# Expert tiles of a vision tower: first product and row turning as pairs over 64 rows, second product over 128

## What is computed

```python
D = 192; M = 768; G = 4; E = 8                       # 32 experts
h = gelu(einsum('nd,edm->enm', xf, W1[g]) + b1[g])   # first product, 192 -> 768
o = einsum('enm,emd->end', h, W2[g]) + b2[g]         # second product, 768 -> 192
y = y + einsum('end,ne->nd', o, combine[:, g, :])    # weighted sum into the token's row
```

## Time and profile before

| | |
|---|---|
| median of 3 runs | 782.18 us |
| span of the profiled execution | 782.1 us (the profile gives no time around it) |
| expert loop, first product of the first tile to that of the last | 399.7 to 768.0 us |
| PE busy in that stretch | 363.5 of 368.3 us |
| typical time from one tile's first product to the next one's | 4.53 us |

### The profile page before, as it was taken

How to read it: one execution, slowest core, us unless ns; L and a number is a source line. 1 busy time by engine, 2 the same in 40 slices (tenths; PEclk the granted TensorE clock), 3 DMA queues, 4 the chain that set the end, 5 groups by cost and what they waited for, 6 DMA issues and landing times.

```text
span 782.1 us, 19902 instructions
## 1 busy us (share of the span) xinstructions
PE 672.5 (86%) x6348; PEld 571.2 (73%) x6348; DVE 426.2 (55%) x1247; ACT 236.5 (30%) x673; POOL 323.5 (41%) x265
## 2 busy tenths in 40 slices
PE   5957858898989996863379899999999999999995
PEld 5724646656745885753269789999999999999994
DVE  7574583745479559977934344444444434434342
ACT  3112312123247211111433333333343333333331
POOL 4730730011023322520334456555564655655554
PEclk9976968577999998975579999999999999999998
DMA  9900000000000030013116765464545665565432
GB/s 349 255 2 3 3 3 2 3 1 3 1 1 1 1 122 1 1 68 132 30 31 164 217 170 116 119 182 81 164 113 161 172 169 161 115 163 114 103 50 38
DMA packets 34982, 70.05 MB, mean 90 GB/s; under 512 B 6353, under 2 KB 21234, under 8 KB 34930
## 3 DMA queue, kind: packets, MB, share of 16 engines
q0 software_dynamic: 15840, 17.71, 13.5%
q10 hardware_dynamic: 8064, 33.12, 12.6%
q1 hardware_dynamic: 11026, 18.48, 7.3%
HBM read 59.31 MB, written 9.98 MB: 89 GB/s over the span
## 4 chain that ended last, share of the span: by engine, by line
PE 62%; DVE 17%; DMA 6%; issue 4%; POOL 1%; ACTq 1%; ACT 1%; DVEq 0%; POOLq 0%
PE bank L1492 17%; PE bank L1484 12%; PE bank L1487 7%; PE bank L1340 4%; PE bank L1469 3%; PE bank L1272 3%; PE bank L1292 3%; DMA arena<-normed_rows,fetch_u 3%; PE bank L1356 2%; DMA out_dram<-arena,number_u 2%; PE bank L1310 1%; PE bank L1283 1%; DVE zx L894 1%; DVE arena L1097 1%; DVE arena L1094 1%
## 5 line engine op out<-in xcount | busy, mean ns | idle before, releaser
L631 POOL DMA_INDIRECT out_dram<-arena,number_u x80 | 127.0, 1587 | 51.6 <-DMA out_dram<-arena,number_u 26.3
L625 POOL DMA_INDIRECT arena<-normed_rows,fetch_u x80 | 78.3, 979 | 114.9 <-DMA out_dram<-arena,number_u 51.0
L1179 DVE COPY arena<-bank 128x256 f32<-128x256 f32 x81 | 34.4, 425 | 119.5 <-PE bank L1469 110.8
L796 ACT ACTIVATE arena<-bank,arena 128x128 f32<-128x128 f32 x234 | 64.5, 375 | 115.5 <-PE bank L1487 115.5
L1492 PE MATMUL bank<-arena 128*128 128x192 f32 x468 | 83.0, 326 | 0.1
L1492 PEld LDWEIGHTS bank<-arena 128*128 128x128 f32 x468 | 75.4, 190 | 0.5 <-ACT arena L796 0.5
L1197 DVE TENSOR_SCALAR arena<-bank,arena 128x192 f32 x80 | 33.4, 418 | 59.1 <-PE bank L1492 57.5
L533 POOL TENSOR_SCALAR rstd<-mv 128x4 f32<-128x4 f32 x12 | 2.7, 229 | 147.5 <-DVE mv L883 147.5
L1484 PE MATMUL bank<-arena 128*128 128x128 f32 x468 | 59.1, 276 | 1.4 <-DVE arena L1179 1.1
L1484 PEld LDWEIGHTS bank<-arena 128*128 128x128 f32 x468 | 56.9, 192 | 3.0 <-issue 1.5
L796 ACT ACTIVATE arena<-bank,w_space 128x128 f32<-128x128 f32 x132 | 36.5, 375 | 67.0 <-PE bank L1487 67.0
(11 more groups left out here) (241 smaller groups left out, 1263.8 us busy)
## 6 DMA issues: line engine op xcount, KB each, us to landing
arena<-in_moe_w_dram ACTq DMA_DIRECT2D x14, 579.0 KB, 6.1
arena<-in_moe_w_dram ACTq DMA_DIRECT2D x14, 576.0 KB, 4.2
arena<-in_xf_dram SPq DMA_DIRECT2D x8, 512.0 KB, 9.8
w_space<-in_moe_w_dram ACTq DMA_DIRECT2D x7, 579.0 KB, 5.8
w2small<-in_moe_w_dram ACTq DMA_DIRECT2D x7, 579.0 KB, 5.6
w_space<-in_moe_w_dram ACTq DMA_DIRECT2D x7, 576.0 KB, 4.2
wab<-in_moe_w_dram ACTq DMA_DIRECT2D x7, 576.0 KB, 4.3
arena<-in_w_dram SPq DMA_DIRECT2D x8, 480.0 KB, 9.1
```

The source lines that it names most:

```text
L625: pool.indirect_dma_start(out=mo_stage[:, s * ROWN:(s + 1) * ROWN], out_offset=None, in_=normed_rows, in_offset=bass.IndirectOffsetOnAxis( ...
L631: pool.indirect_dma_start(out=out, out_offset=bass.IndirectOffsetOnAxis(ap=number_u[:, s:s + 1], axis=0), in_=mo_res[:, s * D:(s + 1) * D] ...
L796: nc.scalar.activation(mo_hT[:, m, :], bank[2 + m][:, 0:P], ACT.Gelu, bias=b1[:, m:m + 1]).then_inc(free[2 + m], 1)
L1179: nc.vector.tensor_copy(mo_xT.rearrange("p k t -> p (k t)"), bank[1][:, 0:2 * P]).then_inc(free[1], 1)
```

## The change

The 192 columns of a row are now three pieces of 64 (`KC` = 3). A token's row is staged twice side by side, so that a turned piece appears on partitions 0 to 63 and again on 64 to 127; tokens 0 to 63 are turned in the upper half of the array and tokens 64 to 127 in the lower, into banks 1 and 6. The first product runs in three pairs: in a pair, one product of 64 rows uses rows 0 to 63 and its partner rows 64 to 127, each summed over three pieces into a bank of its own. Its six results use banks 2, 3, 4, 5, 2, 3, so that the third pair writes banks that the first pair's GELUs must have emptied. The rows of the next tile are turned between the second pair and the third. The second product is as before. DVE takes the columns in two copies, and waits for the third pair before it overwrites `mo_xT`. The weights of the first product have the same number of bytes in another order.

```diff
+ROWS = P // 2
+KC, MP = D // ROWS, MC // 2
+W1N = MP * KC * P
+SUM_BANK, ROW_BANKS, HID_BANKS = 0, (1, 6), (2, 3, 4, 5, 2, 3)
...
+        def hidden_uses(i, m):
+
+            b = HID_BANKS[m]
+            return i * HID_BANKS.count(b) + (moe_base[b] + HID_BANKS[:m].count(b))
...
                 with act.Fori(first, end) as i:
-                    act.wait_ge(full[0], i + moe_base[0])
+                    act.wait_ge(full[SUM_BANK], i + moe_base[SUM_BANK])
                     for m in range(MC):
-                        act.wait_ge(full[2 + m], i + (moe_base[2 + m] + 1))
-                        nc.scalar.activation(mo_hT[:, m, :], bank[2 + m][:, 0:P], ACT.Gelu, bias=b1[:, m:m + 1]).then_inc(free[2 + m], 1)
+                        b = HID_BANKS[m]
+                        act.wait_ge(full[b], hidden_uses(i, m) + 1)
+                        nc.scalar.activation(mo_hT[:, m, :], bank[b][:, 0:P], ACT.Gelu, bias=b1[:, m:m + 1]).then_inc(free[b], 1)
...
             def stage_rows(i):
                 dve.wait_ge(sem("rows_in"), i * 16 + 16)
-                dve.wait_ge(full[1], i + moe_base[1])
+                for b in ROW_BANKS:
+                    dve.wait_ge(full[b], i + moe_base[b])
                 nc.vector.tensor_copy(mo_gates[:, bass.ds(i % 4 * NE, NE)], mo_stage[:, bass.ds(i % STAGE * ROWN + D, NE)])
-                nc.vector.tensor_copy(mo_x[:, D:2 * P], mo_stage[:, bass.ds(i % STAGE * ROWN + P, REST)])
-                nc.vector.tensor_copy(mo_x[:, 0:D], mo_stage[:, bass.ds(i % STAGE * ROWN, D)]).then_inc(sem("rows_staged"), 1)
+                rows = mo_stage[:, bass.ds(i % STAGE * ROWN, D)].rearrange("p (j x) -> p j x", j=KC)
+                nc.vector.tensor_copy(mo_x, repeat(rows, 2, 2)).then_inc(sem("rows_staged"), 1)
 
             def take_columns(i):
-                dve.wait_ge(full[1], i + (moe_base[1] + 1))
-                nc.vector.tensor_copy(mo_xT.rearrange("p k t -> p (k t)"), bank[1][:, 0:2 * P]).then_inc(free[1], 1)
+                for n, b in enumerate(ROW_BANKS):
+                    dve.wait_ge(full[b], i + (moe_base[b] + 1))
+                    nc.vector.tensor_copy(mo_xT[:, :, n * ROWS:(n + 1) * ROWS], bank[b][:, 0:D].rearrange("p (j t) -> p j t", j=KC)).then_inc(free[b], 1)
...
                 with dve.Fori(first, end) as i:
+                    for m in (MC - 2, MC - 1):
+                        dve.wait_ge(full[HID_BANKS[m]], hidden_uses(i, m) + 1)
                     take_columns(i + 1)
                     stage_rows(i + 2)
...
             def transpose_rows(i):
                 pe.wait_ge(sem("rows_staged"), i + 1)
-                for k in range(2):
-                    ins = nc.tensor.transpose(bank[1][:, k * P:(k + 1) * P], mo_x[:, k * P:(k + 1) * P], ident[:])
-                ins.then_inc(full[1], 1)
+                pe.sem_inc(sem("transposing"), 1)
+                for j in range(KC):
+                    for n, b in enumerate(ROW_BANKS):
+                        r = slice(n * ROWS, (n + 1) * ROWS)
+                        ins = nc.tensor.transpose(bank[b][:, j * ROWS:(j + 1) * ROWS], mo_x[r, j].rearrange("p n x -> p (n x)"), ident[r, r])
+                        if j == KC - 1:
+                            ins.then_inc(full[b], 1)
...
+                def hidden_pair(i, p):
+
+                    for m in (2 * p, 2 * p + 1):
+                        pe.wait_ge(free[HID_BANKS[m]], hidden_uses(i, m))
+                    for j in range(KC):
+                        for n in range(2):
+                            r, b = slice(n * ROWS, (n + 1) * ROWS), HID_BANKS[2 * p + n]
+                            ins = mm(bank[b][:, 0:P], w1e[r, p, j, :], mo_xT[r, j, :], start=(j == 0), stop=(j == KC - 1))
+                            if j == KC - 1:
+                                ins.then_inc(full[b], 1)
+
                 with pe.Fori(first, end) as i:
-                    pe.wait_ge(free[1], i + (moe_base[1] + 1))
+                    for b in ROW_BANKS:
+                        pe.wait_ge(free[b], i + (moe_base[b] + 1))
+                    hidden_pair(i, 0)
+                    hidden_pair(i, 1)
+                    transpose_rows(i + 1)
+                    hidden_pair(i, 2)
+                    pe.wait_ge(free[SUM_BANK], i + moe_base[SUM_BANK])
                     for m in range(MC):
-                        mm(bank[2 + m][:, 0:P], w1e[:, m * P:(m + 1) * P], mo_xT[:, 0, :], start=True, stop=False)
-                    for m in range(MC):
-                        r, c = m % 2 * REST, HID + m // 2 * P
-                        mm(bank[2 + m][:, 0:P], w1e[r:r + REST, c:c + P], mo_xT[r:r + REST, 1, :], start=False, stop=True).then_inc(full[2 + m], 1)
-                    transpose_rows(i + 1)
-                    pe.wait_ge(free[0], i + moe_base[0])
-                    for m in range(MC):
-                        pe.wait_ge(free[2 + m], i + (moe_base[2 + m] + 1))
-                        ins = mm(bank[0][:, 0:D], mo_hT[:, m, :], w2e[:, m, :], start=(m == 0), stop=(m == MC - 1))
-                    ins.then_inc(full[0], 1)
+                        pe.wait_ge(free[HID_BANKS[m]], hidden_uses(i, m) + 1)
+                        ins = mm(bank[SUM_BANK][:, 0:D], mo_hT[:, m, :], w2e[:, m, :], start=(m == 0), stop=(m == MC - 1))
+                    ins.then_inc(full[SUM_BANK], 1)
```

More of the change, by code:

```diff
@@ L49 @@
 REST = D - P
-W1N = HID + MC // 2 * P
+ROWS = P // 2
+KC, MP = D // ROWS, MC // 2
+W1N = MP * KC * P
+SUM_BANK, ROW_BANKS, HID_BANKS = 0, (1, 6), (2, 3, 4, 5, 2, 3)
 ROWN = D + NE
@@ L271, in vit_tower @@
         mo_gates = view(P, 4 * NE)
-        mo_x = view(P, 2 * P)
-        mo_xT = view(P, 2 * P).rearrange("p (k t) -> p k t", k=2)
+        mo_x = view(P, 2 * D).rearrange("p (j n x) -> p j n x", j=KC, n=2)
+        mo_xT = view(P, KC * P).rearrange("p (j t) -> p j t", j=KC)
         mo_res = view(P, 2 * D)
@@ L786, in expert @@
                 if e and e + AHEAD - 1 < NE:
-                    act.wait_ge(full[0], first + moe_base[0])
+                    act.wait_ge(full[SUM_BANK], first + moe_base[SUM_BANK])
                     load_expert(act, (u + AHEAD - 1) % AHEAD, e + AHEAD - 1)
@@ L1192, in _ @@
                     new = dve.snap(i % 4 * D)
-                    added, summing = dve.snap(i + 1), dve.snap(i + (moe_base[0] + 1))
+                    added, summing = dve.snap(i + 1), dve.snap(i + (moe_base[SUM_BANK] + 1))
                     half, tile, ahead = dve.snap(i % 2), dve.snap(i + 0), dve.snap(i + 4)
                     nc.vector.tensor_copy(fetch_u[:, bass.ds(half, 1)], table_u[:, bass.ds(ahead, 1)]).then_inc(sem("fetch_set"), 1)
-                    dve.wait_ge(full[0], summing)
-                    ts(out=mo_new[:, bass.ds(new, D)], in0=bank[0][:, 0:D], scalar1=mo_gates[:, bass.ds(gate, 1)], scalar2=None, op0=ALU.mult).then_inc(free[0], 1)
+                    dve.wait_ge(full[SUM_BANK], summing)
+                    ts(out=mo_new[:, bass.ds(new, D)], in0=bank[SUM_BANK][:, 0:D], scalar1=mo_gates[:, bass.ds(gate, 1)], scalar2=None, op0=ALU.mult).then_inc(free[SUM_BANK], 1)
                     dve.sem_inc(sem("scaling"), 1)
@@ L1201, in _ @@
                     nc.vector.tensor_copy(number_u[:, bass.ds(half, 1)], table_u[:, bass.ds(tile, 1)])
-                    dve.wait_ge(free[0], summing)
+                    dve.wait_ge(free[SUM_BANK], summing)
                     nc.vector.tensor_copy(mo_res[:, bass.ds(to, D)], mo_new[:, bass.ds(new, D)]).then_inc(sem("result_ready"), 1)
@@ L1467, in transpose_rows @@
                 pe.wait_ge(sem("rows_staged"), i + 1)
-                for k in range(2):
-                    ins = nc.tensor.transpose(bank[1][:, k * P:(k + 1) * P], mo_x[:, k * P:(k + 1) * P], ident[:])
-                ins.then_inc(full[1], 1)
+                pe.sem_inc(sem("transposing"), 1)
[5 more added lines that the diff above has]
+                            ins.then_inc(full[b], 1)
             tile_starts += [expert_start(pe, e, 1) for e in range(18, 25)]
-            pe.wait_ge(free[1], moe_base[1])
+            for b in ROW_BANKS:
+                pe.wait_ge(free[b], moe_base[b])
             transpose_rows(0)
@@ L1477, in expert @@
                 u = e % AHEAD
[L1478 removed]
+                w1e = mo_w1[u].rearrange("p (m j x) -> p m j x", m=MP, j=KC)
                 w2e = mo_w2[u][:, 0:MC * D].rearrange("p (m d) -> p m d", m=MC)
                 pe.wait_ge(sem(f"in_expert{u}"), 32 * (e // AHEAD + 1))
[L1481 to L1493 removed]
@@ L1495, in _ @@
-            for m in range(MC):
-                pe.wait_ge(free[2 + m], moe_base[2 + m])
+                def hidden_pair(i, p):
[7 more added lines that the diff above has]
+                                ins.then_inc(full[b], 1)
@@ new lines, in expert @@
+                with pe.Fori(first, end) as i:
+                    for b in ROW_BANKS:
+                        pe.wait_ge(free[b], i + (moe_base[b] + 1))
[4 more added lines that the diff above has]
```

(8 more changed lines are left out.)

1 line of the change is left out of this document (removed).

## The result

The kernel after takes 795.29 us, median of four executions (793.32 to 799.75), the kernel before 783.93 us (four, 781.28 to 786.05): a ratio of 1.0172 with the 95% interval 1.0132 to 1.0213, so slower by 1.3 to 2.1%. The forecast was 802 us with a range of 785 to 814. The profiled execution took 794.53 us and has a span of 792.7; before it was 782.1.

A forecast was written before the change was run, and what follows sets the result against it. PE was taken to bound the expert loop, busy 363.5 of 368.3 us. Ordinary tiles +10.4, experts' first tiles +5.9, long issues +5.4 and late starts -2.0 gave +19.7 on 782.1: 802 us, range 785 to 814.

The forecast's parts named there:

- The ordinary tile, +0.13: Each of 80 tiles in the expert loop goes from 4.53 to about 4.67 us on PE, +10.4 us in all.
- eighteen pair slots: First product: 36 half-row records, two started per 0.111 us slot, 18 slots against 18 before; nothing gained or lost.
- the 0.14 for the third pair: Per tile, third pair waits 0.03 to 0.04 us for ACT's GELU 1, then its stream starts afresh, +0.10.
- The expert's first tile, +0.21: ACT issues two DMAs before its first GELU, now wanted at 1.06 but ready at 1.27: 28 times 0.21, +5.9 us.
- The long issues, +5.4: Seven of 28 second DMA issues on ACT run long, 7.1 us over; 1.7 was paid before, now nothing is covered.
- The late adds, 0: DVE's lateness for results POOL had not yet added, four times: absorbed by a slower PE, so 0 us.
- DVE's extra 1.2: DVE's longer copies, paid where it was already late for POOL: +1.2 us, then set to 0.
- The late expert starts, -2.0: PE's idle 2.9 us at eight late expert starts should go, as its queue passes the last GELU earlier: -2.0 us.
- no fresh start at the second product and half the ACT terms: Lower case within the forecast: second product's stream runs on and ACT's costs halve, giving 790 us.
- rival C: First product's half-row pairs cannot be queued two per slot: much slower, 820 to 942 us; chance 0.07.
- Rival A: Neither third pair nor second product starts afresh, ordinary tile 4.47 us: no change, 786 us; chance 0.13.
- Rival B: Form-change costs come from banks handed between forms, so a tile saves 0.30 us: faster, 766 us; chance 0.08.

The follow-up runs named there:

- bank 7: Changed kernel with the fifth result in free bank 7 and the sixth in bank 2, so the third pair waits for the first GELU alone: 786.61 us.
- the kernel without reuse: Changed kernel with second product also in halves, third pair in free columns of banks 1 and 6, no bank reused within a tile: 787.41 us.
- the loads moved: Changed kernel with ACT's two weight DMAs issued behind the GELUs of an expert's last tile instead of ahead of its first: 791.28 us.
- the later GELUs: Changed kernel with the third pair reusing the banks of GELUs 2 and 3, so it waits for GELU 3: 849.42 us.
- split kernels: Changed kernel with the second product also in halves, summed in banks 0 and 3, so PE never changes form: 785.56 us; further variants build on it.
- DVE's loop written out: Changed kernel with second product in halves, DVE's expert loop unrolled and the next expert's start loaded ahead: 779.35 us.
- both edits: Changed kernel with weight DMAs issued behind an expert's last GELUs and the fifth result in bank 7, the sixth in bank 2: 790.15 us.

## Why the prediction came out as it did

**The ordinary tile, +0.13: right,** to 0.01 us (4.66 or 4.67). Its parts: eighteen pair slots at 0.111 stand in the rows (24 records in 1.61, 12 in 0.94), the turning takes 0.18 with nothing in its way, and the second product starts afresh at 2.22. One part was put down to the wrong cause. Of the 0.14 for the third pair, the wait and its restart explain 0.07, as bank 7 shows; the other 0.06 is paid after the turning whether the pair waits or not, and nearly as much where no form changes (0.72 against 0.67 in the kernel without reuse).

**The expert's first tile, +0.21: right** at +0.23, and shown twice: it goes to 0.00 with the loads moved and to 0.04 with bank 7. The cause, ACT's issues ahead of the first GELU, is the one named. A third thing that ACT does there was left out of the sum: its table load in the second tile, +0.5. This term and the ordinary tile's come to 16.7 us, more than the loop's 14.3, so the sign was no luck.

**The long issues, +5.4: mis-sized.** That nothing covers them any more is right (1.26 of 1.32 paid at 705.53). But the prediction took seven of them with 7.1 us over from one execution; the execution after had five with 3.9, and the term came to 2.0. The number varies between executions: bank 7's trace had two (0.60 and 1.53), that of the later GELUs six.

**The late adds, 0: wrong by -4.4.** The prediction said that a slower PE absorbs the lateness but only used it to leave out DVE's extra 1.2; it did not take away the lateness that the profile before had already paid. In the loop of the kernel after none of it is left. DVE's wait for POOL mostly goes with the pace while weights are loaded: none with the later GELUs (tiles of 5.33), 4.4 us in the kernel after, 14.6 to 19.7 in its three variants with first tiles of 4.59 to 4.66, 17.6 before; and none without the weight DMAs. In the split kernels it is 3.7 (first tiles of 5.1), 10.6 (4.84) and, without reuse, 13.1 at 5.0, which does not fit, so there is more to it than pace. Each of these is one execution. That a shorter tile gives back part of its gain to the adds is what they show; how much was not tested by itself.

**The late expert starts, -2.0: right in size**, -2.2 by the tiles. But 0.8 of that are fresh starts behind the idle, which the sum did not name, and four of the late starts (4.75 to 4.82) are still in the trace. No experiment tested it.

**The end of the sum.** 19.7 was forecast for the profiled span and the loop gave 14.3: -3.4 by the long issues, -4.4 by the late adds, +1.3 by the very first tile, whose granted clock was lower, the others within 1. The stretch ahead of the loop took off another 3.7, where the granted clock was higher, which no reading of the loop could tell. Two bounds were added up loosely: no fresh start at the second product and half the ACT terms are 802 - 8 - 5.6 = 788 and not 790, and rival C's 942 sets its 160 on the time before, where on the forecast it is 962. Nothing hangs on either.

**Rival A (786, no fresh starts) fell:** tiles went up, and even with the wait away a tile stays at 4.59, above the 4.53 of before and the 4.47 that A needed. **Rival B (766, the price is the banks', not the form's) fell:** every bank of the hidden layer is begun and finished in one form after the change, yet the price was paid, and it left when the second form left the loop. The sections of the tiles of 4.66 (from 614.83) and 4.27 (from 609.93, with DVE's loop written out) lie side by side: from first to turning 1.44 and 1.34, turning 0.21 and 0.21, third pair to second product 0.87 and 0.77, second product to the next tile 2.14 and 1.95. The first difference is the fresh start of the first product, 0.10; the third is the change into the second product's form, 0.10; the last, 0.19, is the second product's fresh start and the change back. So a form change costs 0.09 to 0.10 and the fresh start behind it 0.10, twice a tile, 0.39 in all. The Trainium skill (TensorEngine Tiling (Array Packing), Key Properties) says that changing the tiling mode drains TensorE; these rows agree and give the price. **Rival C (pairs not overlapping) fell:** 36 half-row records run at 0.056 each.

What stays open: what the 0.06 after the turning is, and why the adds land late beside the weight DMAs; only that they do was shown.

## What to carry to other kernels

Two half-array products side by side gain nothing over one whole product, but each passage between the two forms costs about 0.2 us in this kernel; count the passages, and change all products of a loop or none. Even with one form the gain over the kernel before came only when DVE's passage between experts was off the path, and it is 0.1 to 0.7%. Where a later product reuses a buffer that another engine must empty, ask what that engine does ahead of it (here two DMA issues of 0.8 us), since it comes onto the path. And before a gain is booked, look for the wait that the slower pace was hiding: here adds in DRAM that take longer than a tile while weights are loaded.

## What was not expected of the hardware

- The adds into DRAM, each issued behind the one before, waited up to 3.70 us for it in the row shown and up to 5.21 in the kernel with both edits, beside weight DMAs. Moving the weight DMAs later by an expert's tiles cost the kernel before 0.6%.
- The same issue of a weight DMA on ACT takes 0.46 us or up to 1.78 (2.03 in the split kernel with DVE's loop written out), for the most part in different tiles from one execution to the next.
- DVE's passage between two loops whose bounds it loads shows as 2.62 us of idle time with no releaser; writing the loop out and loading them ahead took it away.
- The first tile of the loop ran at a granted clock of 0.59 in the kernel after and 0.74 before, with periods of 7.49 and 6.10 us. The change alone does not make it so: with the loads moved, the same first tile took 5.93 at 0.76, and with bank 7 7.43 at 0.59. What decides it is open.
